# Another order of all engines in the second stage of a two-layer-stack kernel

## What is computed

```
x = x + attention1(layernorm(x))        # Stieltjes attention, 16 heads of 8, causal, 4 Newton steps
x = x + stack(layernorm(x))               # six times (DEPTH = 6):
    x = attn_layer(shift_tokens(x)) + x     # as written in the reference, per depth i:
        q, k, v = split(x @ Wqkv)           #   16 heads of 64
        q = l2norm(q) * qs; k = l2norm(k) * ks
        q, k = rotary(q), rotary(k)         #   with scale tables
        out = local attention, window 32, each block sees itself and the block before it
        return out @ Wo
    x = ffn_layer(shift_tokens(x)) + x      # layer norm, 128 -> 2 x 341, a * gelu(gate), 341 -> 128
```

## Time and profile before

| | before |
|---|---|
| runs | 4816.96 to 4829.28, median 4825.4 us |
| profiled execution | 4821.14 us, its span 4819.4 us |
| PE busy | 4087.5 us (85%) |
| DVE busy | 3990.3 us (83%) |
| ACT busy | 2994.8 us (62%) |
| POOL busy | 3489.3 us (72%) |
| granted TensorE clock, mean | 0.861 |

### The profile page before, as it was taken

One profiled execution on the slowest core, in us unless ns is written; L12 is line 12 of the kernel. 1 busy time (PEld: TensorE's weight loads), 2 busy tenths in 40 slices (PEclk: granted clock), 3 DMA queues, 4 the chain that ended last, 5 costly groups with the idle time before them and its releaser, 6 DMA issues.

```text
span 4819.4 us, 153868 instructions
## 1 busy us (share of the span) xinstructions
PE 4087.5 (85%) x60260; PEld 2123.1 (44%) x60260; DVE 3990.3 (83%) x7132; ACT 2994.8 (62%) x4240; POOL 3489.3 (72%) x1655
## 2 busy tenths in 40 slices
PE   3666666666655999999999999999999999999997
PEld 1222333223322455555555555555555555555554
DVE  6999999999973788888888888888888888888884
ACT  5999999999982455545554555555555455554552
POOL 4999899999984666667666676666666676666762
PEclk9755555555556999999999999999999999999998
DMA  0000000000003445544445444454454444454443
GB/s 14 3 6 5 10 5 9 5 10 5 3 7 81 101 105 118 118 113 102 111 113 123 109 107 111 118 122 103 103 118 119 113 102 110 118 127 101 107 111 102
DMA packets 230497, 381.82 MB, mean 79 GB/s; under 512 B 38112, under 2 KB 59232, under 8 KB 229728
## 3 DMA queue, kind: packets, MB, share of 16 engines
q1 hardware_dynamic: 229856, 372.57, 32.9%
HBM read 51.57 MB, written 18.61 MB: 15 GB/s over the span
## 4 chain that ended last, share of the span: by engine, by line
PE 47%; issue 5%; DVE 5%; POOL 4%; SPq 3%; DMA 3%; ACT 2%; DVEq 0%; POOLq 0%
PE pb L1396 11%; PE pb L1454 7%; PE pb L1414 6%; PE pb L1437 6%; PE pb L1401 5%; PE pb L1465 3%; PE pb L1448 3%; SPq L1230 3%; PE pb L1477 3%; POOL sqs L1822 3%; DMA qkn<-nf 3%; ACT sq L1674 2%; DVE nf L1957 2%; PE pb L1424 1%; DVE m L1934 1%
## 5 line engine op out<-in xcount | busy, mean ns | idle before, releaser
L734 POOL TENSOR_TENSOR W<-W 128x1280 f32<-128x1280 f32 x416 | 955.5, 2321 | 141.3 <-ACT W L585 139.8
L1822 POOL TENSOR_TENSOR sqs<-sq 128x1024 f32<-128x1024 f32 x192 | 469.3, 2444 | 763.6 <-ACT sq L1674 763.6
L585 ACT ACTIVATE W<-S,lam 128x512 f32<-128x512 f32 (+3 forms) x2048 | 952.3, 554 | 84.0 <-DVE lam L878 72.6
L1826 POOL TENSOR_TENSOR m<-m 128x1024 f32<-128x1024 f32 x384 | 947.3, 2483 | 18.9 <-DVE m L1934 17.4
L849 DVE BATCH_NORM_STATS2 stats<-W 128x6 f32<-128x512 f32 (+3 forms) x2048 | 832.5, 479 | 57.6 <-POOL W L734 56.5
L1396 PE MATMUL pb<-xs,wg 128*128 128x512 f32 x1536 | 733.9, 606 | 14.9 <-DMA xs<-hist 14.5
L1933 DVE TENSOR_TENSOR m<-pb,tab 128x1024 f32<-128x1024 f32 x384 | 467.0, 1216 | 132.9 <-ACT sq L1674 119.9
L1674 ACT ACTIVATE sq<-pb 128x1024 f32<-128x1024 f32 x384 | 393.4, 1025 | 280.0 <-PE pb L1396 279.5
L1957 DVE SCALAR_TENSOR_TENSOR nf<-rn,m 128x1024 f32<-128x1024 f32 x384 | 513.9, 1358 | 53.7 <-POOL m L1826 46.4
L1679 ACT ACTIVATE lnn<-pb,cst 128x1024 f32<-128x1024 f32 x192 | 212.6, 1107 | 496.2 <-PE pb L1401 496.1
L1837 POOL TENSOR_TENSOR pr<-pr,rsum 128x1024 f32<-128x1024 f32 x192 | 365.5, 1904 | 181.1 <-DVE rsum L1970 181.1
(11 more groups left out here) (123 smaller groups left out, 7380.8 us busy)
## 6 DMA issues: line engine op xcount, KB each, us to landing
qkn<-nf SPq DMA_DIRECT2D x1536, 128.0 KB, 2.4
vr<-v SPq DMA_DIRECT2D x96, 768.0 KB, 5.9
vr<-v SPq DMA_DIRECT2D x96, 192.0 KB, 5.5
xr<-hist SPq DMA_DIRECT2D x48, 256.0 KB, 4.8
hist<-xo SPq DMA_DIRECT2D x47, 256.0 KB, 4.9
wg<-wqkv SPq DMA_DIRECT2D x24, 384.0 KB, 3.4
xs<-hist SPq DMA_DIRECT2D x48, 128.0 KB
vr<-v SPq DMA_DIRECT2D x96, 64.0 KB, 6.4
```

The source lines that it names most:

```text
L585: ins = nc.scalar.activation(W[:, p, h, c], S[:, j % 2, h, c], ACT.Abs_reciprocal_sqrt, bias=lam[:, j, i:i + 1])
L734: nc.gpsimd.tensor_tensor(W[:, p, h, :], W[:, p, h, :], W[:, p, h, :], ALU.mult).then_inc(s_wp[p], 1)
L1822: nc.gpsimd.tensor_tensor(sqs[:, :, :], sq[:, :, 0, :], sq[:, :, 1, :], ALU.add).then_inc(s_sqs, 1)
L1826: nc.gpsimd.tensor_tensor(m1[:, which, :, :], m1[:, which, :, :], m2[:, which, ::-1, :], ALU.add)\
```

## The change

The orders of all five engines in the second stage are replaced, the work itself is the same. On PE: `mean` of step b-1 moves from behind k3 of the next body to the end of its body; `variance` moves ahead of q3; v3's matmuls stand behind turn0's (v3's wait stays ahead of them); the second half of weigh2 stands ahead of the first half of score0. Many banks are given anew. So five waits now stand ahead of another run of matmuls (v3 is the new one). On ACT, POOL and DVE some twenty operations change places with their neighbours. On SP: the store moves from two bodies behind to three, near the body's start; the roll of v of the step before goes behind the DMAs of group 3; the waits for Wo, W1, W2 and the vectors move; `load_xr` loads for step b-1 instead of b. The straight bodies ahead of the loops are four instead of three.

```diff
         HOLD = [
-            ("k3", 1, 6), ("mean", 2, 4), ("q3", 1, 0), ("var", 2, 2), ("v3", 1, 4), ("turn0", 1, 2),
-            ("norm3", 1, 6), ("weigh0", 1, 4), ("gate0", 2, 2), ("gate1", 2, 6), ("score2", 1, 4), ("up1", 2, 7),
-            ("q0", 0, 0), ("k0", 0, 4), ("turn1", 1, 6), ("v0", 0, 2), ("weigh1", 1, 6), ("norm0", 0, 4),
-            ("score3", 1, 0), ("v1", 0, 4), ("k1", 0, 2), ("q1", 0, 4), ("turn2", 1, 6), ("up0", 2, 0),
-            ("weigh2", 1, 6), ("norm1", 0, 4), ("score0", 0, 2), ("out", 2, 5), ("turn3", 1, 6), ("q2", 0, 0),
-            ("weigh3", 1, 2), ("k2", 0, 6), ("wo", 1, 2), ("score1", 0, 0), ("norm2", 0, 6), ("v2", 0, 4),
+            ("k3", 1, 6), ("var", 2, 5), ("q3", 1, 0), ("turn0", 1, 2), ("v3", 1, 4), ("norm3", 1, 2),
+            ("weigh0", 1, 0), ("gate0", 2, 2), ("gate1", 2, 6), ("score2", 1, 4), ("up1", 2, 7), ("q0", 0, 0),
+            ("k0", 0, 4), ("turn1", 1, 6), ("v0", 0, 2), ("weigh1", 1, 6), ("norm0", 0, 4), ("score3", 1, 0),
+            ("v1", 0, 4), ("k1", 0, 2), ("q1", 0, 4), ("turn2", 1, 6), ("up0", 2, 0), ("weigh2", 1, 6),
+            ("norm1", 0, 4), ("score0", 0, 2), ("out", 2, 5), ("turn3", 1, 6), ("q2", 0, 0), ("weigh3", 1, 6),
+            ("k2", 0, 2), ("wo", 1, 4), ("score1", 0, 0), ("norm2", 0, 6), ("v2", 0, 2), ("mean", 1, 5),
...
# SP
+                if live(b, 3) and not is_body(b, END + 3):
+                    store(b - 3)
                 if live(b, 0):
                     load_xs(b)
                 if live(b, 1):
+                    rotated(b - 1, 3)
+                if live(b, 1):
                     rolled(b - 1, 1)
...
+                    rotated(b, 1)
                 if live(b, 1):
                     load_w2(b - 1, l, k == 1)
+                if live(b, 1):
+                    load_xr(b - 1)
...
# PE
                 if live(b, 2):
-                    take("mean", b)
-                    residual_due(b - 2)
-                    mean(b - 2, bank("mean"))
-                if live(b, 1):
-                    take("q3", b)
-                    project(b - 1, 3, 0, bank("q3"))
-                if live(b, 2):
                     take("var", b)
                     deviation_due(b - 2)
                     variance(b - 2, bank("var"))
...
+                    take("q3", b)
+                    project(b - 1, 3, 0, bank("q3"))
                 if live(b, 1):
                     take("v3", b)
-                    values(b - 1, 3, bank("v3"))
                 if live(b, 1):
                     take("turn0", b)
                     probabilities_due(b - 1, 0)
                     turn(b - 1, 0, bank("turn0"))
+                if live(b, 1):
+                    values(b - 1, 3, bank("v3"))
...
+                if live(b, 1):
+                    weigh(b - 1, 2, 1, bank("weigh2"))
                 if live(b, 0):
                     take("score0", b)
                     rotated_due(b, 0)
                     scores(b, 0, 0, bank("score0"))
...
+                if live(b, 1):
+                    take("mean", b)
+                    residual_due(b - 1)
+                    mean(b - 1, bank("mean"))
...
-            for b in range(3):
+            for b in range(4):
                 body(b)
...
# DVE
+                    inverse_denominators(b - 1, 2)
                 if live(b, 0):
+                    finish(b, 0, 1)
+                if live(b, 0):
                     finish(b, 0, 0)
...
                 if live(b, 2):
                     finished(b - 2)
+                    mask(b, 0)
+                    finish(b, 1, 1)
+                    finish(b, 1, 0)
+                    weighted(b - 1, 3)
+                    row_max(b, 0)
...
+                    finish(b, 3, 1)
                     mask(b, 2)
-                    finish(b, 3, 1)
                     finish(b, 3, 0)
```

More of the change, by code:

```diff
@@ L1283, in body @@
                 if live(b, 1):
-                    load_wo(b - 1, l, k == 1)
+                    load_w1(b - 1, l, k == 1)
                 if live(b, 0):
@@ L1287, in body @@
                 if live(b, 1):
-                    load_w2(b - 1, l, k == 1)
+                    load_wo(b - 1, l, k == 1)
                 if live(b, 0):
@@ L1291, in body @@
                 if live(b, 1):
-                    load_vectors(b - 1, l, k == 1)
+                    load_w2(b - 1, l, k == 1)
+                if live(b, 1):
+                    load_xr(b - 1)
                 if live(b, 0):
                     rolled(b, 0)
[L1295 to L1298, removed]
                 if live(b, 1):
-                    load_w1(b - 1, l, k == 1)
+                    load_vectors(b - 1, l, k == 1)
             for b in range(BATCH):
@@ L1306, in _ @@
                     body(l * BATCH + k, l, k)
-            for b in range(STEPS, STEPS + 2):
+            for b in range(STEPS, STEPS + 3):
                 body(b, DEPTH, b - STEPS)
@@ L1611, in body @@
                     scores(b, 0, 0, bank("score0"))
-                if live(b, 1):
-                    weigh(b - 1, 2, 1, bank("weigh2"))
                 if live(b, 2):
@@ L1771, in body @@
                 if live(b, 0):
+                    squares(b, 2, 1)
+                if live(b, 0):
                     squares(b, 2, 0)
@@ L1775, in body @@
                 if live(b, 0):
-                    squares(b, 2, 1)
-                if live(b, 0):
                     log_norms(b, 2)
@@ L1780, in body @@
                     inverse_norms(b, 2)
+                if live(b, 1):
+                    squared_deviation(b - 1)
                 if live(b, 0):
@@ L1793, in body @@
                 if live(b, 0):
-                    values(b, 3)
+                    squares(b, 3, 0)
                 if live(b, 0):
@@ L1806, in _ @@
             act.wait_ge(cleared, 1)
-            for b in range(3):
+            for b in range(4):
                 body(b)
-            with act.Fori(3, STEPS) as b:
+            with act.Fori(4, STEPS) as b:
                 body(b)
@@ L1906, in _ @@
             pool.wait_ge(cleared, 1)
-            for b in range(3):
+            for b in range(4):
                 body(b)
-            with pool.Fori(3, STEPS) as b:
+            with pool.Fori(4, STEPS) as b:
                 body(b)
@@ L2061, in body @@
                     weighted(b - 1, 2)
-                if live(b, 0):
-                    finish(b, 1, 1)
+                if live(b, 2):
+                    finished(b - 2)
                 if live(b, 0):
@@ L2072, in body @@
                 if live(b, 0):
+                    row_max(b, 0)
+                if live(b, 0):
+                    rotate(b, 2, 0)
+                if live(b, 0):
                     rotate(b, 2, 1)
                 if live(b, 0):
-                    rotate(b, 2, 0)
-                if live(b, 2):
-                    finished(b - 2)
-                if live(b, 0):
                     denominators(b, 0)
+                if live(b, 1):
+                    residual(b - 1)
                 if live(b, 0):
@@ L2082, in body @@
                 if live(b, 1):
-                    residual(b - 1)
+                    centre(b - 1)
                 if live(b, 0):
@@ L2087, in body @@
                     finish(b, 2, 0)
-                if live(b, 1):
-                    centre(b - 1)
                 if live(b, 0):
@@ L2123, in _ @@
             tables(0)
-            for b in range(3):
+            for b in range(4):
                 body(b)
-            with dve.Fori(3, BATCH) as b:
+            with dve.Fori(4, BATCH) as b:
                 body(b)
```

46 lines of the change are left out of this document (20 added, 26 removed).

## The result

The changed kernel takes 4886.5 us (median of 4 runs, 4878.0 to 4890.0), the kernel before 4821.2 in the same comparison (4 runs): ratio 1.0134, interval 1.0122 to 1.0147. The forecast was 4844. The sign was right; the loss is 1.34%, where 0.38% was forecast. The profiled execution took 4878.0 us, its span 4876.1, which is 56.7 us more than before.

The account below looks back on a forecast made before the run. PE was taken to set the time, with only gaps of some 2.2 us a body to save. 14 (40 bodies at +0.35) + 6.8 - 2.4 = +18.4 us on the 4825.4 median gave 4844 us, range 4814 to 4890.

Parts of the forecast that it names:

- The sign: Whole kernel: forecast slower, +18.4 us (+0.38%); chance of slower by more than a measurement can tell, 0.55.
- Parts 1 and 2: q3 to turn1: q3 behind var makes norm3 0.91 us later, its gap 1.2; port delays finishes, turn1 0.6 later.
- Parts 3 and 4: score3 to out: DMAs make score3, k1 and q1 0.57 us later, out 0.35 later; +0.35 us a body.
- parts 1 to 4: Steady body, from mean and var through turn1 and score3 to out: +0.35 us a body, +14 us over some 40.
- rival B: Group 0's finishes on DVE: POOL's normalise(2) takes the port between them, out 1.4 us later a body, 4886 us; chance 0.2.
- Part 6: Store, SP's order and end: moved store, loads and waits cost nothing; y lands earlier at the end, -2.4 us.
- part 4's lower bound: Steady body's sum: at best -0.3 us, with the port free, DMAs landing earlier ahead of the roll, and gaps shrinking.
- Part 5: Straight bodies ahead of the loops: one more costs the whole difference from a loop body, +6.8 us, lower end 0.
- The end, -2.4: Last step: y lands by 4787, PE starts the gates at about 4788.6 instead of 4790.95; -2.4 us, other end 0.

Follow-up runs that it names:

- f3_roll0: Changed kernel with DVE's finishes in old order, half 1's v roll ahead of group 3's DMAs again, half 0's held until v2's matmuls finish: 4816.4 us, 0.9994.
- f7_roll0only: Changed kernel with half 1's v roll ahead of group 3's DMAs again and half 0's held until v2, finishes left in new order: 4842.5 us, 1.0047.
- e2_roll: Changed kernel with only the v roll of the step before put ahead of group 3's DMAs again on SP: 4869.3 us, 1.0098.
- e10_rollback: Kernel before with only the v roll of the step before moved behind group 3's DMAs on SP: 4893.4 us, 1.0158.
- e5_four: Kernel before with four straight bodies ahead of the loops instead of three, nothing else: 4819.8 us, 0.9997.
- e8_edge: Changed kernel with finishes and half 1's v roll undone, and mean moved to the first thing behind the loop's jump, ahead of score1: 4895.4 us, 1.0173.
- f1_finishback: Kernel before with only group 2's reciprocal and finish(0,1) put ahead of finish(0,0) on DVE: 4835.1 us, 1.0040.

## Why the prediction was wrong, step by step

**Parts 1 and 2, the chain of norm3.** The gap came out as forecast, 1.16 to 1.2 us, released by sqs; turn1's gap went. The two later finishes met POOL as forecast (1.84 and 1.78 us in the body shown, against 1.22 undisturbed and 2.1 forecast for the first). In f3_roll0 norm3 starts at T 21.33 against 20.55 before (medians): 0.78 us later, where 0.91 was forecast.

**Parts 3 and 4, score3 to out, +0.35 a body.** Right as far as it goes. In f3_roll0, with the rolls and the port out of the way, out starts at T 56.90 against 56.56 before: 0.34 us later, where 0.35 was forecast; 0.19 of it is given back by the body's end, which leaves +0.15. (f3_roll0 also has the hold, so this isn't a clean price of parts 1 to 4.) One reading of the row was wrong: in the body of the earlier trace rows PE wasn't held at score3 (3061.97 has no idle time ahead of it). It was held just before, in weigh1, for issue:

```profile
3061.38 0.25 PE L1437 MATMUL pb<-pT,v 64*64 64x32 f32 x3 [0.24 <-issue]
```

That is a small case of the stops above: it stands five times in the kernel before, and PE goes on 1.4 to 1.6 us after a piece has landed. And rival B's port, at chance 0.2, was the true case: it is 0.6 of the 1.8 us (f7_roll0only against f3_roll0), 0.27 alone in the kernel before. I had argued against it that no row showed a POOL instruction waiting between two finishes; the row at 3078.67 shows DVE waiting and getting the port as POOL's instruction ended, and it works the same way for POOL. The Trainium skill ("SBUF — State Buffer", section "SBUF: two separate sides") has this as a lock held for the whole instruction; the 4.96 us for two finishes with a 2.88 us normalise ending in between agree. B's 4886 us hit the time by luck: undone in this order, the measured 1.8 a body are 1.0 of rolls, 0.6 of port and 0.15 of the rest.

**Part 6, SP's order: this is the step that failed.** It priced the moved store, loads and waits at nothing and had the roll only as a possible gain, in part 4's lower bound ("DMAs land earlier because the 1 MB roll of v now stands behind them"). The two rolls cost 44 us (after against f7_roll0only), 1.0 us a body; the one of half 1 alone costs 1.58% in the kernel before. I asked who waits for the roll's result and for q/k's, not what else uses the DMA engines meanwhile. PE's own instructions do. Two things show that the fetch is the link: each stop goes when its roll goes (e2_roll, f3_roll0) or comes when it comes (e10_rollback), and each of these stops and each jump ends at a nearly fixed distance behind the landing of an instruction piece, which starts when the roll's data run out. Why that distance is about 1.4 us is open, and no run moved the fetch by itself.

**Part 5, one more straight body, +6.8.** Wrong: e5_four shows 0.9997. The body from 1600.87 is long, but not for being straight: the next straight one takes 67.4 us in e5_four. Its 2.62 us stop is a roll's too. The roll is issued at 1625.82, a piece starts at 1630.44 (T 29.6), and PE goes on 1.38 us after its landing. In e10_rollback, with the same code on PE and this roll 13 us later in the body, the same piece starts at T 24.7, the stop is gone, and this body takes 68.77 us instead of 73.74. So I had the fetch stop in my rows and took it for a price of straight code. For this term the Trainium skill's rule ("Runtime: NRT & Kernel Launch", section "Instruction fetch mechanics") gave the better figure, nothing. Its reason, that a taken branch waits for the fetch of its target, agrees with the jumps here, 0.9 to 4.5 us (medians). It also says that crossing a 16 KiB block in straight code is mostly hidden. In the kernel before that is so (scores wait 0.9 us for issue in three times), but not for a run of small matmuls behind a roll: there the traces have a median stop of 1.2 us (after) and 1.3 us (e10_rollback).

**The end, -2.4.** Right: y isn't waited for, the gates follow xn (4850.11 + 0.77) at once, and the stretch behind the last out-projection is 3.2 us shorter. The waits answer to the earlier trace rows:

```profile
4850.11 0.77 POOL L1848 TENSOR_SCALAR xn<-xc,vec 128x512 f32<-128x512 f32 x1 [25.01 <-DVE xc L2010]
...
4851.03 4.51 PE L1465 MATMUL pb<-xn,w 128*128 128x512 f32 x6 [2.81 <-POOL xn L1848]
```

The stretch up to the first dense body, 9.9 us shorter after (6.4 in e5_four), was in no part, and I did not look for its cause.

## What to carry to other kernels

A large DMA that nobody waits for can still stop an engine that runs many small instructions: look where the transfers lie against the runs of small matmuls and against a loop's jump, and when PE stops for "issue" in the middle of equal small matmuls, look whether an instruction piece has just landed. Price every moved DMA by what else uses the engines in its new place. When undoing one part changes nothing, undo it again with the other suspect out of the way: two parallel waits hide each other.

## What the runs showed of the hardware

- A jump back of PE's loop took 0.89 us (median) in f3_roll0, 1.6 to 1.7 in the kernel before with and without the roll held, 2.7 in the kernel after behind the roll, 4.5 in e8_edge. In all five it ended 1.35 to 1.70 us after an instruction piece of 16,384 bytes had landed.
- A run of 64 small matmuls (0.79 us) stopped in its middle for 0.3 to 1.9 us (59 stops in after and e10_rollback) where a roll of 1 MB had been issued ahead of the instruction piece: the piece started 4.5 to 6.8 us after the roll's first DMA, and PE went on 1.2 to 1.6 us after its landing.
- When two of DVE's finishes (SCALAR_TENSOR_TENSOR on two SBUF tensors) follow each other directly and POOL's normalise waits, POOL gets the port between them: 4.0 to 5.0 us for the two, median 4.95, instead of 2.4, in 37 or 38 pairs in each of three kernels (after, f1_finishback, f7_roll0only).
